# An audio block on one core: x rows loaded in two transfers, the square root table loaded ahead, and unread products added on TensorE

## The reference

```python
amp = jnp.abs(jnp.fft.rfft(x, axis=1))                       # 188 bins
src = jnp.concatenate([x[:, -1:, :], amp], axis=1) + pos      # 189 tokens
src = layer_norm(src + mha(src)); src = layer_norm(src + ff(src))
tau = clip(softplus(mha2(src)[:, -1:]) / 10, 0.01, 1.0)
h = weighted window sum of x, weights tau ** seq              # (8, 344, 64)
X = layernorm(h)
h = h + ((rope(X @ W_Q) @ rope(X @ W_K).T) * decay) @ (X @ W_V)
h = h + product_key_attention(layernorm(h))                   # 8 heads x 8 batches
```

## Time and profile before

| | us |
|---|---|
| median of 3 runs | 1924.92 |
| lowest and highest run | 1922.6, 1926.18 |
| the profiled execution, own time | 1926.57 |
| its span in the trace | 1924.8 |
| TensorE busy | 1867.0 |
| mean granted clock | 0.987 of full speed |

### The profile page before, as it was taken

One profiled execution on the slowest core, in us unless ns is written; L12 is line 12 of the kernel. 1 busy time (PEld: TensorE's weight loads), 2 busy tenths in 40 slices (PEclk: granted clock), 3 DMA queues, 4 the chain that ended last, 5 costly groups with the idle time before them and its releaser, 6 DMA issues.

```text
span 1924.8 us, 43767 instructions
## 1 busy us (share of the span) xinstructions
PE 1867.0 (97%) x11488; PEld 1408.0 (73%) x11488; DVE 1608.8 (84%) x4825; ACT 1459.5 (76%) x2969; POOL 1317.6 (68%) x1576
## 2 busy tenths in 40 slices
PE   7997899999999999999999999999999999999997
PEld 5765577777777777777777777777777777777775
DVE  4646788888888888888888888888988888888886
ACT  3853488877878777888887778887887787878885
POOL 1112377777777777777777777777777777777775
PEclk8998899999999999999999999999999999999998
DMA  3001110001000200011000200020001100020001
GB/s 110 2 1 48 58 22 21 21 16 61 20 21 21 63 17 17 21 52 33 21 16 17 63 21 21 21 61 17 19 21 32 54 16 17 18 65 21 21 19 28
DMA packets 118622, 58.00 MB, mean 30 GB/s; under 512 B 110224, under 2 KB 116560, under 8 KB 117261
## 3 DMA queue, kind: packets, MB, share of 16 engines
q1 hardware_dynamic: 115778, 56.75, 11.4%
q10 hardware_dynamic: 2795, 0.70, 0.2%
HBM read 24.55 MB, written 0.70 MB: 13 GB/s over the span
## 4 chain that ended last, share of the span: by engine, by line
POOL 42%; issue 38%; PE 7%; POOLq 2%; DVE 1%; SPq 0%; ACT 0%; DMA 0%; DVEq 0%; ACTq 0%
POOL k_W_low L1409 25%; POOL k_aS L1351 3%; POOL k_cand L1365 2%; POOL k_ecs L1395 2%; POOL k_tab_low L1414 2%; PE ps L990 2%; POOL k_aS L1358 2%; PE ps L981 1%; PE ps L998 1%; POOL k_aS L1356 1%; POOLq L1408 1%; POOL k_small L1380 1%; POOL k_small L1381 1%; POOL k_ecs L1376 1%; POOL k_off L1385 1%
## 5 line engine op out<-in xcount | busy, mean ns | idle before, releaser
L1409 POOL TENSOR_TENSOR k_W_low<-k_W,k_W_high 128x688 fp32r<-128x688 f32 x513 | 851.2, 1659 | 320.9 <-ACT k_W_high L1223 317.6
L1218 ACT ACTIVATE k_W<-ps 128x688 f32<-128x688 f32 x1029 | 770.0, 748 | 339.6 <-PE ps L981 327.2
L1575 DVE SCALAR_TENSOR_TENSOR k_W<-ps,k_W 128x688 f32<-128x688 f32 x1028 | 887.9, 866 | 162.9 <-ACT k_W L1218 152.6
L990 PE MATMUL ps<-k_W,k_tab 128*128 128x344 f32 x2048 | 676.4, 453 | 0.0
L981 PE MATMUL ps<-k_X,sel 128*128 128x344 f16 x2058 | 472.4, 311 | 17.1 <-DMA k_X<-k_spl 9.0
L990 PEld LDWEIGHTS ps<-k_W,k_tab 128*128 128x128 f32 x2048 | 366.2, 190 | 126.9 <-issue 0.2
L1223 ACT ACTIVATE k_W_high<-k_W 128x688 fp32r<-128x688 f32 x513 | 398.0, 776 | 0.8
L998 PE MATMUL ps<-k_W_high,k_tab_high 128*128 128x344 f32 x1024 | 386.2, 380 | 0.0
L981 PEld LDWEIGHTS ps<-k_X,sel 128*128 128x128 f16 x2058 | 164.6, 98 | 237.6 <-issue 77.1
L998 PE MATMUL ps<-k_W_high,k_tab_low 128*128 128x344 f32 x1024 | 323.9, 319 | 0.0
L1002 PE MATMUL ps<-k_W_low,k_tab_high 128*128 128x344 f32 x1024 | 246.6, 322 | 0.0
(11 more groups left out here) (237 smaller groups left out, 2308.9 us busy)
## 6 DMA issues: line engine op xcount, KB each, us to landing
k_tab<-in_tables SPq DMA_DIRECT2D x9, 2048.0 KB, 7.2
k_X<-k_spl SPq DMA_TRANSPOSE x390, 2.3
k_xs<-x2T SPq DMA_DIRECT2D x66, 86.0 KB, 2.0
k_qT<-k_qs SPq DMA_DIRECT2D x33, 86.0 KB, 2.0
cst<-in_consts SPq DMA_DIRECT2D x1, 1024.0 KB, 10.0
wts<-in_weights SPq DMA_DIRECT2D x1, 896.0 KB, 7.6
cst<-in_consts SPq DMA_DIRECT2D x1, 874.5 KB, 6.0
xr<-in_xrows SPq DMA_DIRECT2D x1, 750.0 KB
```

The lines of the kernel that those rows point to most:

```text
L990: mm = mm_(sums, tab[:, slot, at + k, :], W[:, d % RING, k, :], start=(d == 0 and k == 0), stop=(d == NDC - 1 and k == 1))
L1218: A(W[:, d % RING, :, :], ps[:, 2 * (d % 2):2 * (d % 2) + 2, 0:LOUT], ACT.Exp).then_inc(e_done, 1)
L1409: G.tensor_tensor(W_low[:, q % SPLIT_RING, :, :], W[:, d % RING, :, :], W_high[:, q % SPLIT_RING, :, :].bitcast(F32), ALU.subtract).then_i ...
L1575: V.scalar_tensor_tensor(W[:, d % RING, :, :], ps[:, 2 * (d % 2):2 * (d % 2) + 2, 0:LOUT], 0.0, W[:, d % RING, :, :], ALU.is_ge, ALU.mult) ...
```

## The change

Four edits. The x rows are loaded as rows 0 to 111 and rows 112 to 124, both counting into the same semaphore, which is now awaited at 32 on SyncE and TensorE. The unread products ahead of the transform are 16 in place of 12. ScalarE loads the table set of the square root by name before it waits for the transform. TensorE does four unread products of 344 columns into bank 3 between the values and the first retention scores, once the four sine products of the queries are done.

```diff
-                sp_.dma_start(xr[:, :, :].rearrange("p c n -> p (c n)"), xrows.rearrange("p c b d -> p (c b d)")).then_inc(s_x, 16)
+                for r0, r1 in ((0, 112), (112, XROWS)):
+                    sp_.dma_start(xr[r0:r1, :, :].rearrange("p c n -> p (c n)"), xrows[r0:r1].rearrange("p c b d -> p (c b d)")).then_inc(s_x, 16)
                 sp_.dma_start(cst[:, 0:d1], consts[:, 0:d1]).then_inc(s_dft, 16)
-                sp_.wait_ge(s_x, 16)
+                sp_.wait_ge(s_x, 32)
...
-                for _ in range(12):
+                for _ in range(16):
                     mm = nc.tensor.matmul(ps[:, 7, 0:128], zeros[:, 0:128], zeros[:, 0:128], start=True, stop=True)
                 mm.then_inc(warm_done, 1)
-                pe.wait_ge(s_x, 16)
+                pe.wait_ge(s_x, 32)
...
+                nc.scalar.preload_act_table_set("sqrt_and_others")
                 for p in range(NPAIR):
                     act.wait_ge(dft_done, p + 1)
...
                     mm.then_inc(v_mm, 1)
+
+                pe.wait_ge(sin_done, 4)
+                for _ in range(4):
+                    mm_(ps[:, 3, 0:LOUT], const("mean"), x2T[:, 0, :], start=True, stop=True)
```

## The result

| | before | after |
|---|---|---|
| median, us | 1924.38 (4 runs) | 1936.47 (4 runs) |
| lowest and highest | 1922.6, 1926.18 | 1933.36, 1938.58 |
| the profiled execution, its span | 1926.57, 1924.8 | 1936.33, 1934.5 |

The ratio of after to before is 1.006 (95% interval 1.0047 to 1.0072): the change makes the kernel 12 us slower, where 7.5 us less were forecast, and 1936 lies far outside the range.

A forecast was written before the change was run, and what follows sets the result against it. TensorE was taken as 97% busy, with the first 200 us one chain of engines waiting for each other. Gains of 3.8 + 1.7 + 0.9 + 1.1 = 7.5 us off the median 1924.92 gave 1917.4, range 1913.8 to 1921.3.

The forecast's parts named there:

- Part 3: Before the square root: naming its table set early removes a 1.28 us load; the root starts 0.9 us sooner.
- (c): Rival at the x load: 112 rows spread over fewer than five DMA engines, giving 1928.9 us; chance 3%.
- Split: At the x load: 112 rows use all sixteen DMA engines; transform starts at 8.0 instead of 11.84, gaining 3.8 us.
- rival (a): At the x load: the split does not spread it, five engines still carry it; 1922.9 us; chance 7%.
- Clock of the transform: At the transform: shorter TensorE idle with sixteen unread products keeps the clock at 1.00, gaining 1.7 us (0 to 1.84).
- Table of the root: At the square root: no table load between squares and root, which waits only for the last sum; 0.9 us.
- Queries' clock: At the queries: clock may still fall after a 2.9 us gap; counted as nothing, up to 1.7 us if it holds.
- rival (d): At the queries: the clock holds there as well, giving 1915.7 us; chance 18%.
- Products ahead of the scores: Between values and scores: four unread products keep TensorE's clock at 1.00, gaining 1.1 us (0 to 1.5).
- Rival (b): After the front: gains partly given back as 1.2 GHz stretches fall elsewhere; 1920.5 to 1921.3 us; chance 12%.

The follow-up runs named there:

- experiment 5: The changed kernel with one unread copy of a column added on ScalarE behind the named table load: 1917.42 us, ratio 0.9955.
- experiment 3: The kernel before with the named table load alone added: 1944.07 us, ratio 1.0101.
- experiment 9: The kernel before with two ScalarE copies of projected values merged into one with one increment, TensorE waiting for 3 instead of 4: 1945.7 us.
- experiment 12: The kernel before with the x rows loaded in two transfers and nothing else changed: 1920.7 us, ratio 0.998.
- experiment 6: The changed kernel with four unread copies of a column added on ScalarE behind the named table load: 1917.87 us, ratio 0.9953.
- experiment 7: The changed kernel with five unread copies of a column added on ScalarE behind the named table load: 1916.89 us, ratio 0.9953.
- experiment 10: The changed kernel with sixty copies of one column added on ScalarE ahead of the squares: 1914.4 us, ratio 0.9949.
- experiment 2: The changed kernel with an increment of a semaphore nobody waits for added behind the named table load: 1935.87 us, ratio 1.0053.
- experiment 8: The kernel before with two ScalarE copies of projected values merged into one with an increment of 2: 1926.85 us, ratio 1.0005.

## Why the prediction was wrong

**The step that failed** is the premise "The main loop from about 224 us on is untouched by the change". None of its operations is changed, but where its code lies is. Part 3 said that "The named load takes the place of the one ScalarE does at 0.73, idle time", and costed that at nothing; true of the time at 0.73, but the load of line 432 went as well, and that takes one instruction out of ScalarE's stream. It cost 19 to 22 us: 19.1 by the medians of after and experiment 5 (1936.47 and 1917.42), 20.4 with each set against the runs of before beside it (12.1 more than 1924.38, 8.3 less than 1925.75), 22.1 by their loops (1692.4 and 1670.3), 19.5 and 18.7 by the loops of experiments 3 and 9 against before's 1672.2. No rival of the prediction held it either; (c), the slower one, was another mechanism.

How the idle stretch becomes 7 us a return: in before a return costs 1.9 us already (27.59 + 26.47 = 54.06 against 26.5 + 25.7 for an ordinary pair), with VectorE's wait of 2.8 to 3.1; after the change it costs 8.7 (60.91), with ScalarE's 7.7. The 6.8 us at half clock behind it are part of the 8.7. Experiment 3 lets their share be estimated: at its second return ScalarE waits 7.44 us, as after does at its own second (7.49), but the clock is low for 3.4 us only (1082.2 to 1085.6, against 1072.3 to 1079.2), and the two rounds take 59.55 us in place of 60.91. So 3.4 us at half clock are worth about 1.4, and 6.8 us about 2.7 of the 8.7.

The trace agrees in kind with the Trainium skill (Runtime: NRT & Kernel Launch, section on the mechanics of instruction fetch): an engine holds two blocks of its code, and a taken branch to a target outside them has to fetch before it goes on. The section gives blocks of 16 KiB; the packets that go with these waits have 8192 bytes, and the fetches stand some 128 instructions apart. Where a loop begins then decides whether its head is still held at its end; here a shift by one instruction costs 7 us a return.

**Part by part**, against the forecast:
- Split: a start at 8.45 (8.0 forecast, bounds 7.4 to 8.7), a gain of 3.4 us instead of 3.8. Experiments 5 and 12 started at 7.97 and 7.89. Right; rival (a) is out, with a DMA share of 1.00 from 3 to 5 us.
- Clock of the transform: the first square is 4.96 us earlier, 1.57 of it by the clock (1.7 forecast). Right in size; but the idle stretch was 2.19 us and not 1.4, and by experiment 12 the four added products have no share in it.
- Table of the root: from the square's 4.96 us to 5.85 at the root and at the queries, 0.9 as forecast. The root did not wait for more than its sum, and before's row without a drain behind a table load was the right one to go by.
- Queries' clock: it held in after, rival (d): TensorE's next stages gain 1.7 us on top (the output projection starts at 108.61 instead of 116.15, 7.54 earlier). It is no sure gain: experiment 5 starts the queries at 18.69 after the same gap of 2.90 us, and from 20.0 to 23.0 its clock is 0.50; in the traces of experiments 6, 7 and 10 it falls there too. That it held in after was luck. No rule for this fell out of the runs.
- Products ahead of the scores: the similarities gain 1.3 us more than the scores (8.86 to 7.54); 1.1 was forecast.
- Behind that the front wins still more: 10.5 us at the first gains copy, as one slow stretch fewer lies there. Rival (b), giving back by slow stretches elsewhere, did not come in after's front. It shows in experiment 6, whose first gains copy is at 229.2, 3.7 us behind after's, with slow stretches at the queries, from 213.2 to 216.6 and from 220.0 to 226.8.

So with the loop's code in its old place the forecast stands: experiments 5, 6 and 7, with all four edits, took 1917.42, 1917.87 and 1916.89 us; 1917.4 had been the number. That it agrees so closely is in part luck: experiment 5 gains 8.3 us on the before of its own round, and in its trace 8.8 us at the first gains copy and 1.9 in the loop (1670.3 against 1672.2), which no part of the sum had.

**Open**: the three blocks within which a loop stays at hand, and their 128 instructions, are read from where the fetches stand, not tested. Heads behind 317, 320 and 321 instructions are well, 376 costs a fetch that is hidden, 316 and 315 cost the wait. By this reading 322 should still be well and 323 should fetch; places between 321 and 376 and below 315 were not tried. Experiment 10 is 2.5 us below experiment 7 by the medians, but they ran beside different runs of before (1924.49 and 1925.75); the ratios, 0.9949 and 0.9953, do not differ.

## What to carry to other kernels

In a kernel whose loop about fills what an engine holds of its code (here 379 instructions of ScalarE), an edit ahead of the loop can have a second price: it moves the loop's head in the instruction stream of its engine, and here one instruction was worth 20 us. After such an edit, compare the number of instructions of each engine ahead of the loop, look at the row of instruction fetches and at idle time "<-issue" where the loop returns, and if there are new ones, put in an idle instruction or two and look again. Before dropping an edit whose whole is slower, see whether its parts gained where they should: here 10 us were there, and one copy of a column took away the loss that hid them.

## What the runs showed of the hardware

- ScalarE's branch back took 0.25 us with the code at hand and 2.6 to 2.8 us with a fetch; with a border right behind the target it was 7.3 to 8.3 us until the code behind the border ran.
- ScalarE's loop of 379 instructions showed no fetches after its first turn with its head behind 317 to 321 instructions, and five on every later turn behind 315, 316 or 376. The later of them stand 120 to 134 instructions apart.
- The number of fetches (31, 46, 47 packets) doesn't tell the cost: 46 packets went with 1936.5 us and with 1914.4.
- A semaphore increment of its own and a wait may or may not be instructions: experiment 2 added none, experiment 8 removed none.
- TensorE's clock fell to 0.50 after 4.41 us without work at the return, in the middle of a loop that is otherwise at 1.00, and stayed there for 6.8 us.
